# The own rows of a four-layer graph network in the stages B to E: made by ScalarE in pieces of 64 columns, in place of one VectorE instruction

## The reference

```python
h = jnp.maximum(_layernorm(x, axis=-1), 0.0)
x = x + _L0_gnn_ref(h, edge_attr_32, src, dst, ...)   # attention over the edges of a target
h = jnp.maximum(_layernorm(x, axis=-1), 0.0)
x = x + _L1_gnn_ref(h, src, dst, ...)                 # one convolution
h = jnp.maximum(_layernorm(x, axis=-1), 0.0)
x = x + _L2_gnn_ref(h, edge_index, ...)               # two convolutions, with self loops
h = jnp.maximum(_layernorm(x, axis=-1), 0.0)
x = x + _L3_gnn_ref(h, edge_index, ...)               # two convolutions, with self loops
```

## Time and profile before

| what | value |
|---|---|
| median of 3 runs | 2498.05 us (2489.75 to 2498.25) |
| the profiled execution, its own time | 2492.77 us |
| its span | 2491.0 us |
| granted TensorE clock, mean | 0.881 of full speed |
| DVE busy | 1880.8 us, 76% of the span |
| PE busy | 1800.8 us, 72% |
| POOL busy | 1773.3 us, 71% |
| ACT busy | 1299.9 us, 52% |

### The profile page before, as it was taken

The page is one execution under the profiler, slowest core; times in us unless marked ns, Lnnn a source line. Parts: engine busy times, 40 slices in busy tenths (PEclk is TensorE's granted clock), DMA queues, the critical chain, the costliest instruction groups (busy, mean ns, idle before and its releaser), DMA issues.

```text
span 2491.0 us, 25939 instructions
## 1 busy us (share of the span) xinstructions
PE 1800.8 (72%) x6414; PEld 870.1 (35%) x6414; DVE 1880.8 (76%) x3066; ACT 1299.9 (52%) x2694; POOL 1773.3 (71%) x1776
## 2 busy tenths in 40 slices
PE   3888888855995788878888878868888888860000
PEld 1433344322543344434444334333444344430000
DVE  6999998647888578987999789887999799960000
ACT  2767676524885455545666456546666566630000
POOL 6777777767777777727776377747777377777776
PEclk9999999877998899979999899879999899985555
DMA  3344433234775454434444356654444354440000
GB/s 70 97 127 128 127 115 89 71 93 146 239 242 185 128 165 124 127 112 104 120 120 118 96 165 188 183 172 107 124 116 123 104 136 134 132 140 22 23 22 20
DMA packets 223225, 302.21 MB, mean 121 GB/s; under 512 B 78896, under 2 KB 85165, under 8 KB 222952
## 3 DMA queue, kind: packets, MB, share of 16 engines
q1 hardware_dynamic: 166632, 249.64, 30.8%
q0 software_dynamic: 56448, 50.92, 11.1%
HBM read 156.13 MB, written 144.91 MB: 121 GB/s over the span
## 4 chain that ended last, share of the span: by engine, by line
DVE 21%; PE 18%; POOL 18%; issue 13%; ACT 6%; DMA 1%; DVEq 0%; POOLq 0%; SPq 0%; ACTq 0%
POOL mn_ring L527 10%; POOL out_dram L1883 8%; PE bank L1195 5%; DVE mn_total L1573 5%; DVE node_h L1401 4%; PE bank L1199 3%; PE bank L1204 3%; PE bank L1927 3%; PE bank L1189 2%; DVE node_h L1446 2%; PE bank L1209 2%; DVE mn_scaled L1589 1%; ACT node_square L1322 1%; ACT node_std L1306 1%; DVE node_x L1425 1%
## 5 line engine op out<-in xcount | busy, mean ns | idle before, releaser
L527 POOL DMA_INDIRECT mn_ring<-slot_rows,addr_i x980 | 969.6, 989 | 445.8 <-issue 293.9
L1195 PE MATMUL bank<-node_x,center 128*128 128x512 f32 x492 | 251.8, 626 | 75.9 <-DVE node_h L1401 71.7
L1204 PE MATMUL bank<-node_h,wconv 128*128 128x512 f32 x492 | 268.3, 628 | 0.3 <-DVE mn_sums L1713 0.3
L1199 PE MATMUL bank<-node_square,mean 128*128 128x512 f32 x492 | 265.3, 622 | 3.7 <-ACT node_std L1301 3.0
L527 POOL DMA_INDIRECT found<-node_table,look_i x196 | 209.4, 1068 | 74.9 <-issue 62.8
L1322 ACT ACTIVATE node_square<-bank 128x512 f32<-128x512 f32 x246 | 145.9, 593 | 210.7 <-PE bank L1195 210.6
L1316 ACT ACTIVATE node_act<-bank,bias 128x512 f32<-128x512 f32 x246 | 168.4, 685 | 148.7 <-PE bank L1204 148.5
L527 POOL DMA_INDIRECT xin<-in_x_dram,src_i x192 | 194.6, 1013 | 64.3 <-issue 57.6
L1883 POOL DMA_INDIRECT out_dram<-keep,scat_i x196 | 193.5, 987 | 62.6 <-issue 62.6
L527 POOL DMA_INDIRECT xin<-in_x_dram,dst_i x192 | 196.0, 1021 | 58.5 <-issue 58.5
L1209 PE MATMUL bank<-node_act,wconv 128*128 128x512 f32 x442 | 229.5, 602 | 2.5 <-ACT node_act L1316 2.5
(11 more groups left out here) (337 smaller groups left out, 3820.8 us busy)
## 6 DMA issues: line engine op xcount, KB each, us to landing
out_dram<-node_rows SPq DMA_DIRECT2D x98, 256.0 KB
mn_rin<-res SPq DMA_DIRECT2D x96, 256.0 KB, 3.8
slot_rows<-node_rows SPq DMA_DIRECT2D x96, 256.0 KB
slot_rows<-keep SPq DMA_DIRECT2D x96, 256.0 KB, 2.0
mn_fcol<-f_rows SPq DMA_DIRECT2D x192, 128.0 KB, 4.0
res<-mn_x SPq DMA_DIRECT2D x72, 256.0 KB, 3.0
node_x_in<-in_x_dram SPq DMA_DIRECT2D x64, 256.0 KB, 3.0
mn_ring<-slot_rows,addr_i POOLq DMA_INDIRECT x980
```

The lines of the kernel that those rows point to most:

```text
L527: return eng.indirect_dma_start(out=dest, out_offset=None, in_=table, in_offset=bass.IndirectOffsetOnAxis(ap=index, axis=0))
L1195: pe.matmul(bank[i][:, :], C["center"][:, :], src, start=True, stop=True).then_inc(s["centered"][i], 1)
L1199: pe.matmul(bank[4][:, :], C["mean"][:, :], nd.square[:, i - 1, :], start=True, stop=True) \
L1204: pe.matmul(bank[5 if i == 2 else 1][:, :], C["wconv"][:, 2 * i - 4, :], nd.h[i][:, u % 2, :], start=True, stop=True) \
```

## The change

The multiplication that makes the own rows is taken from DVE in the stages B to E: one instruction of 128 by 512 with the factors broadcast along the features (lines 1605 and 1656). ACT makes them in their place, one activation `Copy` for each tile of 64 columns with the column of `f2m` as its scale, eight for a group; the last one raises `row`. In B and D they stand on ACT after `deviation`, ahead of `rest(t)`, and wait for the group's `h`; in C and E they stand at the start of the iteration after the group's, ahead of `begin(t)`, and wait for PE's `back`. In C to F DVE's `gather_sum` now waits for `row` of the same group in the stage before.

```diff
@@ gather_sum (DVE) @@
                     else:
+                        v.wait_ge(s["row"], i - 2 * n + 1)
                         v.tensor_tensor(here, here, of_group(keep, g), ALU.add).then_inc(s["gs"], 1)
@@ finish (DVE) @@
+                    if st in "CE":
+                        return
                     v.wait_ge(s["back"], i + 1)
-                    if st in "CE":
-                        v.tensor_tensor(group3(keep, g), rows3(out, g), scale(C["f2m"], g), ALU.mult) \
-                            .then_inc(s["row"], 1)
-                        return
@@ normalise (DVE) @@
                     v.wait_ge(s["h"], i + 1)
-                    if st in "BD":
-                        v.tensor_tensor(group3(keep, g), rows3(hb, g), scale(C["f2m"], g), ALU.mult) \
-                            .then_inc(s["row"], 1)
@@ ACT @@
+                def own_rows(st, g):
+                    i = at(st, g)
+                    if st in "CE":
+                        act.wait_ge(s["back"], i + 1)
+                        act.wait_ge(s["gs"], i + 1)
+                        source = bank[7]
+                    else:
+                        act.wait_ge(s["h"], norm_at(st, g) + 1)
+                        if st == "D":
+                            act.wait_ge(s["gs"], i + 1)
+                        source = h[:, i % 2, :]
+                    for j in range(tiles(g)):
+                        t = 2 * GP * g + j
+                        last = act.activation(keep[:, t * F:t * F + F], source[:, j * F:j * F + F], ACT.Copy,
+                                              scale=C["f2m"][:, t:t + 1])
+                    last.then_inc(s["row"], 1)
+
                 for i, (st, g) in enumerate(order):
                     if st == "A" and g > 0:
                         squares(norm_at(st, g - 1), g - 1)
+                    if st in "CE" and g > 0:
+                        own_rows(st, g - 1)
...
                     if st in NORMS and g > 0:
                         deviation(norm_at(st, g - 1), g - 1)
+                    if st in "BD" and g > 0:
+                        own_rows(st, g - 1)
                     if st in "CEF":
                         mix(i, st, g)
+                    if st in "CE" and g == n - 1:
+                        own_rows(st, g)
                     if st in NORMS and g == n - 1:
                         squares(norm_at(st, g), g)
                         deviation(norm_at(st, g), g)
+                        if st != "A":
+                            own_rows(st, g)
```

## The result

| | before | after |
|---|---|---|
| median (lowest to highest) | 2498.15 us (2489.75 to 2499.78, 4 runs) | 2545.2 us (2538.3 to 2549.8, 4 runs) |
| ratio, 95% interval | | 1.0193 [1.0158, 1.0227] |
| profiled execution, span | 2491.0 us | 2548.0 us |
| granted clock, mean | 0.881 | 0.873 |

The kernel is slower by 47 us, and its median is 2 us under the 2547 us of the forecast.

The account below looks back on a forecast made before the run. DVE's chain was taken to bound B, DVE and POOL's gathers D, a loop through PE C and E. B +26.6, D +22.9 and tails +1 made +50 on 2492.8: 2543 us profiled, median 2547, range 2518 to 2574.

Parts of the forecast that it names:

- The bound: DVE's chain in B, DVE and POOL's gathers nearly equal in D, a loop through PE without the removed instruction in C and E.
- The price of a piece: On ACT a piece takes 0.342 us and starts every 0.244, so eight hold ACT for 1.95 us.
- rival 1: Pieces are cheap, 1.25 us for eight, and PE's clock stays up: +20 us, 2517 in all; chance 0.15.
- rival 2: Eight pieces take 2.74 us (2572 us), or PE's low clock comes in every B and D tick (2560); chance 0.17.
- A tick of D: In D's tick iterations the second L1401 comes 2.28 us later, at T + 5.61; with PE's low clock 2.5 taken.
- A tick of B: In B's tick iterations +1.7 us, or 2.6 if PE's clock falls; 2.1 taken.
- Iterations without a tick: DVE saves the removed instruction: -0.61 us each, in 8 iterations of B and 8 of D.
- C and E: Pieces hide under ACT's wait for PE with 0.7 us to spare; the distance from scan to scan changes by 0 us.
- The gathers of D: Of DVE's 9.1 us of ring waits for POOL in D, 7.7 go, and about 2 of slow PE with them.
- The terms of B: Stage B as a whole: 15 ticks at 2.1 us less 8 other iterations at 0.61, +26.6 us.

Follow-up runs that it names:

- e4_hole: Changed kernel with the eight pieces of B's and D's tick iterations moved behind ACT's copy L1372: 2479.07 us, 0.9939 of the kernel before.
- e2_ce_only: Changed kernel with the own rows of B and D back on DVE, only C and E on ACT: 2494.26 us, 1.0001 of the kernel before.
- e5b_fill: Changed kernel plus two unread PE products ahead of the gap in D's ticks, on a slow chip: 3156.98 us against 3123.93 before, 1.0092.
- e6c_double_ce: Changed kernel with each piece of C and E made twice, first into a spare tile: 2568.23 us, 1.0281 of the kernel before.
- e1_bd_only: Changed kernel with the own rows of C and E back on DVE, only B and D on ACT: 2547.4 us, 1.0204 of the kernel before.
- e7b_hole_ce_dve: Kernel of e4_hole with the own rows of C and E back on DVE, on a slow chip: 3120.03 us against 3123.93 before, 1.0002.

## Why the prediction was right

**The bound.** In B and D DVE does set the pace: e4_hole frees it there and gains. In C and E it doesn't: e2_ce_only gives 0, and the distance changed by 0.06 us where 0.61 us of DVE work left.

**The price of a piece.** Forecast 0.342 us with a start every 0.244. The trace has 332 ns in the middle and eight in 2.02 us, so (2.02 - 0.33) / 7 = 0.24 apart:

```profile
L2025 ACT ACTIVATE keep<-mn_h,f2m x392: 331/332/349, 858.8 to 1736.4; 128x64 f32<-128x64 f32 x196
...
L2025 ACT ACTIVATE keep<-bank,f2m x392: 305/324/362, 1175.6 to 2021.8; 128x64 f32<-128x64 f32 x196
```

(One line of code by its two forms: shortest, middle and longest in ns.) The column as scale costs what the column as bias did, so rival 1, the cheap piece, fell, and with it the dear piece of rival 2. The other half of rival 2, the low clock in every tick of B and D, came true in D and in seven of the 15 ticks of B. The Trainium skill (ScalarE: Activation LUTs, What ACT_TABLE_LOAD costs) gives 186 ns, 93 more for an operand read through a pointer, and 0.833 a column, which makes an estimate of 186 + 93 + 64 x 0.833 = 332 ns; the trace agrees for a pointer scale too, with 332 in the middle.

**A tick of D.** Forecast for the second L1401 T + 5.61, found T + 5.59; for the scans +2.5, found +2.75. The way over ACT, 2.28, was right, and the lower clock, put at 0 to 0.6 with 0.2 taken, is 0.48 (e5b_fill). PE's wait for L1356 was forecast at 3.3 us and is 2.50: ACT is as late as forecast, but PE's work ahead of it, L1209, starts at T + 0.28, where it started at T - 0.58. The sum doesn't use this number, only that the wait is long.

**A tick of B.** Forecast +1.7 without the fall of the clock, 2.6 with it, taken 2.1. Of the eight later ticks seven add 1.58 to 1.67, without the fall behind PE's gap of 1.9 to 2.3 us, and the eighth adds 2.79, with it. That puts most of them at 13.60 to 13.71 us, just under the 13.8 to 14.6 of the forecast. The seven early ones add 1.6 to 4.6, 19.2 us together. There local units are copied by L1339 and not L1356, PE's gap is 1.9 to 3.4 us, and behind six of the seven the clock fell. The timeline of one of them in the changed kernel:

```profile
861.35 1.12 PE L1189 MATMUL bank<-ident,node_h 128*128 128x128 f32 x4 [2.46 <-ACT node_rows L1339]
...
862.25 1.91 PE L1209 MATMUL bank<-node_act,wconv 128*128 128x512 f32 x2
```

I had read one iteration of B and taken it for all 15. The mean of all 15, 2.24, came near the 2.1 taken, by luck as much as by the bounds.

**Iterations without a tick.** Forecast -0.61 each. Nine of the 16 have -0.60 to -0.62; the others lie between -0.94 and +0.34, and together they are -7.5 and not -9.8 us.

**C and E.** Forecast 0 with 0.7 us to spare, found -0.06 an iteration with 0.97 to spare; e6c_double_ce puts the room at 1.1. What I hadn't foreseen is 3.8 us less in C. Of it 2.2 are in the first iteration alone (17.51 to 15.29), where DVE waits 4.8 us for the ring and not 6.2, and 0.5 in the last but one; the rest is spread. e1_bd_only has most of this too.

**The gathers of D.** Forecast that of 9.1 us of ring waits 7.7 go; 4.4 went. By the distances more went: in the kernel before, five iterations with a tick were longer than 11.35 by 10.7 us together, for whatever reason, and in the changed one the ticks exceed 14.10 by only 1.9. So D grew by 15 x 2.75 = 41.3 less 8.7 in the ticks, 3.3 in the iterations without one and 0.6 in the first: 28.6. The 8.7 are near the forecast's 9.7 (7.7 of ring waits and 2 of slow PE), but how much of them is the ring's was not tested apart.

So the mechanism held, and the sum came near: +50 forecast on the span, +57 found in the one profiled execution, +47 in the medians. The terms of B (+26.6, found +30.2) and D (+22.9, found +28.6) were both too small, by 3.6 and 5.7 us; in D the lower clock, taken at 0.2 and not 0.48 a tick, makes most of it, and C's 3.8 less offset a part. That the median was met within 2 us is luck: the profiled execution of the changed kernel is the slowest of its four, 4.6 us over their median, and that of the kernel before 5.3 under its own. (The forecast's own terms give 2543 + 5.3 = 2548, where it writes 2547.)

## What to carry to other kernels

Before work is moved to the emptier engine, look at where in its order it will stand and what stands behind it: the same eight instructions cost 2 percent ahead of a chain that two engines wait for, nothing in C and E, and stood some instructions later in the same queue in a version that is 0.6 percent faster than the kernel before. Look too at what waits for the moved work to be done: there the later store held up a load behind it. A late instruction is paid for again where PE loses its clock in the gap that it makes (0.48 us a tick here). And read every kind of iteration before one is multiplied by fifteen.

## What the runs showed of the hardware

- A piece with its source in PSUM takes 305 to 362 ns and eight end after 1.75 us, so they start 0.20 us apart; from SBUF 0.24. In a row of ACT instructions without a break single ones look longer (L1316 0.81 us in e6c_double_ce, 0.74 in the change, 0.69 in the kernel before) and the next still starts 0.57 behind.
- PE's granted clock fell to its lower level behind all 15 gaps of 2.50 to 4.52 us ahead of L1189 in D of the changed kernel. It stayed up behind gaps of 1.89 to 2.31 us in seven later ticks of B, but also behind one of 2.83 us there, and in e5b_fill behind the 1.14 us shown. So the length of a gap alone doesn't tell which; what else decides was not tested.
- Two chips ran the unchanged kernel at 3147 and 3124 us in place of 2495 to 2498. Busy times account for little of it: POOL's gathers take 968.3 us in e7b_hole_ce_dve and 986.0 in e4_hole, DVE is busy for 1855.2 and 1824.6 us; PE, at a mean clock of 0.803 against 0.883, for 1951.6 and 1794.4. The time goes into waits, which lengthen many iterations by 7 to 8 us and some by up to 20. The chain that ended last, first in e4_hole, then in e7b_hole_ce_dve:

```profile
DVE 20%; PE 18%; POOL 15%; issue 13%; ACT 8%; DMA 3%; SPq 0%; DVEq 0%; POOLq 0%; ACTq 0%
```

```profile
issue 16%; PE 15%; another core or an unknown queue 14%; DVE 13%; ACT 9%; POOL 6%; DMA 0%; DVEq 0%; SPq 0%; POOLq 0%; ACTq 0%
```

  The 14 percent that the profile can't name stand nowhere in the first. Iterations without a stall had the usual distances (11.25, 13.61 or 14.09, 6.76, 7.46). What stops the engines there wasn't tried and stays open.
